# An eight by eight product in front of the output projection and of the down projection of a transformer layer

## The reference

```python
q, k, v = (split_heads(x @ w + b) for w, b in ((wq, bq), (wk, bk), (wv, bv)))
scores = einsum('bhqd,bhkd->bhqk', q, k) * 48 ** -0.5 + adj[:, None]
ctx = einsum('bhij,bhjd->bhid', softmax(scores), v)          # heads side by side again
x1 = rmsnorm(x + ctx @ wo + bo, alpha1, gamma1)              # 384 x 384
y = rmsnorm(x1 + silu(x1 @ w1 + b1) @ w2 + b2, alpha2, gamma2)  # 384 x 1536, 1536 x 384
out = layernorm(x + y)
```

## Time and profile before

| | |
|---|---|
| median of 3 runs | 2911.36 us (2911.35 to 2911.66) |
| profiled execution | 2910.08 us, its span 2908.3 us |
| PE busy / its weight loads | 99% / 98% of the span |
| DVE / ACT / POOL busy | 63% / 49% / 24% |
| PE matmuls in the trace | 25216 |
| granted clock of PE, mean | 0.998 |

### The profile page before, as it was taken

How to read it: one execution, slowest core, us unless ns; L and a number is a source line. 1 busy time by engine, 2 the same in 40 slices (tenths; PEclk the granted TensorE clock), 3 DMA queues, 4 the chain that set the end, 5 groups by cost and what they waited for, 6 DMA issues and landing times.

```text
span 2908.3 us, 62626 instructions
## 1 busy us (share of the span) xinstructions
PE 2882.5 (99%) x25216; PEld 2841.8 (98%) x25216; DVE 1846.2 (63%) x3621; ACT 1431.3 (49%) x4259; POOL 684.3 (24%) x968
## 2 busy tenths in 40 slices
PE   7999999999999999999999999999999999999998
PEld 7999999999999999999999999999999999999998
DVE  6766666656666566566665666666656666566564
ACT  5544545445445454454544544545445445454452
POOL 0222222221222222212222222222221222222222
PEclk9999999999999999999999999999999999999999
DMA  5211212112112121121221211212112112121110
GB/s 172 76 54 57 65 43 68 56 50 64 54 57 65 41 70 52 53 65 48 63 59 47 66 54 56 64 43 68 56 49 64 54 57 65 41 70 53 52 47 28
DMA packets 155490, 171.93 MB, mean 59 GB/s; under 512 B 18624, under 2 KB 155200, under 8 KB 155200
## 3 DMA queue, kind: packets, MB, share of 16 engines
q1 hardware_dynamic: 151952, 166.92, 19.7%
q10 hardware_dynamic: 3248, 0.99, 0.2%
HBM read 92.35 MB, written 25.17 MB: 40 GB/s over the span
## 4 chain that ended last, share of the span: by engine, by line
PE 97%; DVE 1%; DMA 1%; SPq 1%; ACT 0%; issue 0%; POOL 0%; ACTq 0%; POOLq 0%; DVEq 0%
PE ps_work L443 48%; PE ps_rows L581 27%; PE ps_rows L443 7%; PE ps_att L514 4%; PE ps_att L470 4%; PE ps_work L495 2%; PE ps_work L499 2%; PE ps_att L451 1%; PE ps_work L451 1%; SPq L359 0%; DMA x_in<-in_x 0%; DVE w_s L802 0%; DMA stage<-in_L_gnn_wq 0%; POOL x_in L413 0%; DVE neg_max L827 0%
## 5 line engine op out<-in xcount | busy, mean ns | idle before, releaser
L443 PE MATMUL ps_work<-x1T,w_s 128*128 128x256 f32 x6912 | 821.9, 280 | 1.8 <-ACT h_raw L714 1.8
L443 PEld LDWEIGHTS ps_work<-x1T,w_s 128*128 128x128 f32 x6912 | 819.3, 188 | 2.2 <-ACT h_raw L714 2.2
L581 PE MATMUL ps_rows<-w_s,h 128*128 128x384 f32 x4608 | 815.0, 337 | 0.0
L581 PEld LDWEIGHTS ps_rows<-w_s,h 128*128 128x128 f32 x4608 | 796.2, 188 | 0.0
L714 ACT ACTIVATE h_raw<-ps_work,b_col 128x256 f32<-128x256 f32 x768 | 322.3, 471 | 533.1 <-PE ps_work L443 524.9
L660 ACT ACTIVATE probs<-probs,neg_max 128x128 f32<-128x128 f32 x1024 | 396.4, 391 | 190.3 <-DVE neg_max L827 190.3
L425 POOL TENSOR_TENSOR x<-x,rows 128x768 f32<-128x768 f32 x64 | 117.5, 1836 | 1160.8 <-DVE h L885 1160.8
L689 ACT ACTIVATE squares<-y 128x384 f32<-128x384 f32 x128 | 67.1, 524 | 627.8 <-DVE y L894 627.8
L883 DVE CAST h<-h_raw 128x512 fp32r<-128x512 f32 x384 | 163.8, 427 | 249.0 <-ACT h_raw L714 248.8
L894 DVE TENSOR_TENSOR y<-ps_rows,x 128x384 f32<-128x384 f32 x128 | 71.4, 558 | 385.0 <-PE ps_rows L581 385.0
L885 DVE TENSOR_TENSOR h<-h_raw,h 128x512 fp32r<-128x512 f32 x384 | 265.9, 692 | 13.2
(11 more groups left out here) (75 smaller groups left out, 3439.2 us busy)
## 6 DMA issues: line engine op xcount, KB each, us to landing
x_in<-in_x SPq DMA_DIRECT2D x128, 384.0 KB, 3.2
qk<-qk_flat SPq DMA_DIRECT2D x381, 96.0 KB, 2.3
x_last<-in_x SPq DMA_DIRECT2D x64, 384.0 KB, 3.7
out<-y SPq DMA_DIRECT2D x63, 384.0 KB, 2.7
bias<-in_adj SPq DMA_DIRECT2D x64, 128.0 KB, 2.1
qk<-qk_flat SPq DMA_DIRECT2D x127, 64.0 KB, 2.0
qk<-qk_flat SPq DMA_DIRECT2D x127, 32.0 KB, 2.0
stage<-in_L_gnn_w SPq DMA_DIRECT2D x17, 192.0 KB, 4.0
```

The source lines that it names most:

```text
L443: mm = pe.matmul(ps_out, stationary(sta), moving(mov), start=(i == 0), stop=(i == n - 1))
L581: mm = pe.matmul(ps_rows[b][:, 0:d], h[:, sta, m, b * P:(b + 1) * P], w2_s[:, mov, m, :], start=(m == 0 and i == 0), stop=(m == fc - 1 and ...
```

## The change

A new function `short_product` issues one matmul: stationary and moving operand are both the first eight columns of wo_s (high part, block 0; 128 rows, float32r). Its result, 8 x 8, goes to ps_rows0, partitions 0 to 7, columns 384 to 391, which nothing reads. `output_product` issues it for b = 0 after the wait for res2_ready[0] and before the wait for ctx_lo[0]. `down` issues it for b = 0 after the wait for res1_ready[0] (or res2_ready[0]) and before the first wait for h_lo. Nothing else changes, on PE or elsewhere. Four lines come in above, so later lines have higher numbers.

```diff
+            def short_product(ps_out):
+
+                pe.matmul(ps_out, wo_s[:, HI, 0, 0:8], wo_s[:, HI, 0, 0:8], start=True, stop=True)
+
...
             def output_product(g, b):
                 if live(g + LAG_ATTN - LAG_FF - 1):
                     pe.wait_ge(res2_ready[b], through(g + LAG_ATTN - LAG_FF - 1))
+                if b == 0:
+                    short_product(ps_rows[0][0:8, 384:392])
                 pe.wait_ge(ctx_lo[b], through(g))
...
                     pe.wait_ge(res1_ready[b], through(g + LAG_FF - LAG_ATTN))
                 elif live(g - 1):
                     pe.wait_ge(res2_ready[b], through(g - 1))
+                if b == 0:
+                    short_product(ps_rows[0][0:8, 384:392])
                 for m in range(fc):
```

## The result

| | before | after |
|---|---|---|
| median | 2911.65 us | 2918.24 us |
| lowest and highest of 14 runs | 2910.31 to 2913.53 us | 2915.99 to 2919.20 us |
| ratio, 95% interval | | 1.0021 (1.0013 to 1.0029) |
| profiled execution / span | 2910.08 / 2908.3 us | 2918.73 / 2916.9 us |
| one full slot | 44.89 us | 45.00 us |

The change costs 6.6 us. I had forecast 26.9.

A forecast was written before the change was run, and what follows sets the result against it. TensorE's stream was taken to bound the kernel; 0.110 us (output projection) plus 0.310 (down projection) made 0.420 per slot, times 64 26.9 us, added to the 2911.36 us median: 2938.3 us, range 2926 to 2946.

The forecast's parts named there:

- What bounds the kernel: Whole kernel: TensorE, busy 99% of the span; whatever is added to its stream is added some 64 times over.
- The price of a section change: On TensorE, a change of array shape: 0.093 us empty, then the exposed first load, 0.107 for 128 columns, 0.03 for 32.
- That the short product changes the section: Before both projections: the eight column product takes section 128*32, unlike its neighbours 48*128 or 128*128 in front and 128*128 behind.
- The output term: Before the output projection: one more emptying, 0.093 us, plus 0.017 for the short product, 0.110 us added per group.
- rival 2: Eight columns count as no shape change: output 0.017, down 0.114 us per group, 8.4 us in all, 2919.8; chance 5%.
- The down term: Before the down projection: two emptyings of 0.093 us, short product 0.017, big load 0.107 exposed; 0.310 us added per group.
- the lost cover: Down projection's first big load, until now hidden beside the last transpose, stands exposed: 0.107 us per group.
- The short pair: The short product's load (0.01 us) and step (0.007) at both places: 0.017 us, ends 0.007 and 0.14.
- The tests named in advance: Signs around the short product: slots of 45.31 us; a following load within 0.03 us, or a one-sided 0.09 gap, refutes the forecast.
- rival 3: Output's big load runs beside the emptying, gaining 0.09 us per group: 2912.9, no change (4%), or 2905.6, faster (2%).
- The waits: res2_ready (or weight_split) and res1_ready move from the big product to the short one; nothing newly held, no term.

## Why the prediction was wrong

- **What bounds the kernel**: right. TensorE's stream alone sets the time; every nanosecond found in a slot came back 60 to 64 fold in the medians (107 ns and 6.6 us, 440 and 28.2, 200 and 12.1).
- **The price of a section change**: right. 0.093 us of empty array and then the exposed load by its columns; the plain float32 run, which has the section changes that I foresaw, added it up to 28.2 us, where I had 26.9.
- **That the short product changes the section**: this step failed, and both terms with it. I took the section from the name that the built program gives it, 128*32, and bore it out by the context products, the only narrow ones in the trace. Those are plain float32; the short one is float32r, and no row of before shows a float32r product with fewer than 128 columns. I noted that a change of type costs nothing in the earlier trace rows and did not ask whether the type decides the section. Width and type stood on different rows, and I carried one over to the other.
- **The output term**, 0.110 forecast, -0.007 measured. With no second emptying it was to be 0.017 by rival 2. The short load is 8 ns, the short matmul's own step hides beside the big load, and the stream behind runs 15 ns faster through its first matmuls.
- **The down term**, 0.310 forecast, 0.113 measured. Of its four parts the lost cover (0.107) is the only one that is real. I wrote that the loss of cover "makes it", though it was a third of my sum.
- **The short pair**, 0.017 forecast: the load is 8 ns (I had 10), the step 27 ns (I had 7). The Trainium skill's page "TensorEngine Tiling (Array Packing)", Instruction Overhead, was nearer with its estimate of 25 ns than my line through two rows. The step is hidden in both places behind the 128 column load that follows.
- **The rivals**: rival 2 is what happened. It said 8.4 us and 2919.8; measured 6.6 and 2918.24. It had 5% and lay outside the range. Part of its nearness is luck: its down term is 0.114 with a step of 0.007 in it, while the step is 27 ns and hidden, and its output term is 0.017 where the slot shrank by 0.007. Its "against" was the built program's name for the section, which is no row of the trace.
- **The tests named in advance** settled it at once: the load behind the short product follows within 0.03 us in the output projection, which I had given as the sign of rival 2 or 3. It comes 0.21 us after the last score matmul, for 0.20 before, so the gain of rival 3, 0.09 us, is not there. I had the output projection's mean staying at 343 ns and the down projection's rising by 1.5; they are 341 and an unchanged 337, so these means, whose ends are modelled, were no good sign.
- **The waits** that moved cost nothing, as said.

## What to carry to other kernels

A cost rests on the whole form of a row: before a product is priced by a neighbour's row, its type, rows, columns and position have to agree, and where one does not, the range should go to the case in which that one decides. In a stream whose loads are covered, a tiny product is dear by the load that it uncovers (109 ns here), not by its own size; at a section change, where nothing is covered, it is almost free if its own section is that of one of its neighbours (-7 to 14 ns), and costs one emptying more if it is that of neither (103 ns).

## What the runs showed of the hardware that I had not expected

- A float32r product of 8 or 32 columns behaved as one that takes all columns of the array: no emptying next to 128*128 products (109 and 108 ns in front of the down projection, all of it the uncovered load), while the same 8 columns in plain float32 had two (328 ns) and 128 columns in plain float32 none (223 ns, two loads). Rows count in either type (64 rows: 296 ns).
- A transpose's load was through in 0.06 us, a product's of the same 128 columns in 0.108.
- A short matmul of 8 moving columns occupied 27 ns.
- What stands in front of a stream of big products changes its steps for long after. From the last score matmul to the first q matmul, the same matmuls took 3.48 us with a float32r product ahead of the scores, 3.45 in the kernel before and 3.43 with the plain float32 product ahead of the scores; with the short product in between they took 3.44. In the slowest case the q and k projections were slower too; all three together took 96 ns more over 72 matmuls. Between the fastest and the slowest lie 47 ns, more than the 8 ns that an added product's load costs there. The cause is open.
